# A graph layer's node stage: rows loaded and stored two blocks at a time, and a pause behind every second early gather

## The reference

```python
h = jnp.maximum(_layernorm(x, axis=-1), 0.0)                 # x: 100000 x 64, float32
edge_in_f = concat([h[src], h[dst], edge_attr])              # 25000 edges, src random, dst sorted
msgs_f = relu(edge_in_f @ W1_f + b1_f) @ W2_f + b2_f
agg = segment_sum(msgs_f, dst, num_segments=n_nodes)
edge_in_r = concat([h[dst], h[src], edge_attr])
msgs_r = relu(edge_in_r @ W1_r + b1_r) @ W2_r + b2_r
agg = agg + segment_sum(msgs_r, src, num_segments=n_nodes)
out = x + h + relu(concat([agg, h]) @ Wn1 + bn1) @ Wn2 + bn2
```

## Time and profile before

| | us |
|---|---|
| median of 3 runs | 1609.94 |
| lowest, highest | 1607.84, 1611.34 |
| the profiled execution | 1610.51 |
| its span, first to last instruction | 1608.8 |

### The profile page before, as it was taken

The page is one execution under the profiler, slowest core; times in us unless marked ns, Lnnn a source line. Parts: engine busy times, 40 slices in busy tenths (PEclk is TensorE's granted clock), DMA queues, the critical chain, the costliest instruction groups (busy, mean ns, idle before and its releaser), DMA issues.

```text
span 1608.8 us, 29477 instructions
## 1 busy us (share of the span) xinstructions
PE 1280.4 (80%) x7070; PEld 970.6 (60%) x7070; DVE 972.0 (60%) x3294; ACT 942.1 (59%) x2256; POOL 1103.2 (69%) x1003
## 2 busy tenths in 40 slices
PE   5899998457877778887787877778888756899998
PEld 4677777335655555665565656556666544666665
DVE  7999999426666666666666666666666641222222
ACT  4888888345555555555545555555555524677776
POOL 7888888888888888888888888888888761000000
PEclk9999999768788887778778788887777887999999
DMA  6899998425555555555555555555555547999998
GB/s 214 288 312 315 312 316 290 141 51 111 109 111 111 111 105 104 104 105 105 104 104 105 105 102 100 103 103 103 104 102 101 101 71 235 345 353 343 347 342 298
DMA packets 238410, 281.00 MB, mean 175 GB/s; under 512 B 53170, under 2 KB 155200, under 8 KB 238348
## 3 DMA queue, kind: packets, MB, share of 16 engines
q1 hardware_dynamic: 168408, 241.57, 45.2%
q0 software_dynamic: 68992, 38.59, 20.5%
q10 hardware_dynamic: 948, 0.30, 0.1%
HBM read 162.62 MB, written 117.72 MB: 174 GB/s over the span
## 4 chain that ended last, share of the span: by engine, by line
POOL 33%; issue 22%; DMA 15%; PE 4%; DVE 3%; ACT 1%; POOLq 0%; SPq 0%; DVEq 0%; ACTq 0%
POOL table L532 28%; DMA out_x<-ncentred 12%; POOL got_odd L514 6%; DMA table<-to_send,scatter_at 2%; DVE ncentred L1138 2%; DVE same L979 1%; PE bank L833 1%; PE bank L871 1%; DMA same<-table 1%; PE bank L820 1%; PE bank L882 0%; PE bank L818 0%; SPq L392 0%; PE bank L804 0%; PE bank L892 0%
## 5 line engine op out<-in xcount | busy, mean ns | idle before, releaser
L532 POOL DMA_INDIRECT table<-to_send,scatter_at x392 | 622.6, 1588 | 134.0 <-issue 118.4
L846 PEld LDWEIGHTS bank<-message,same 128*128 128x128 f32 x1960 | 270.3, 222 | 44.2 <-issue 39.2
L846 PE MATMUL bank<-message,same 128*128 128x128 f32 x1960 | 290.9, 313 | 4.8 <-DVE message L1011 4.8
L639 ACT ACTIVATE nh<-nx,all_sums,all_rstd 128x64 f32<-128x64 f32 x784 | 280.2, 434 | 0.1
L514 POOL DMA_INDIRECT got_even<-in_x,gather_first x196 | 212.9, 1086 | 39.8 <-issue 34.7
L775 PE MATMUL bank<-wn_h,nturned 128*128 128x256 f32 x784 | 196.7, 394 | 31.7 <-ACT nhidden L683 24.1
L514 POOL DMA_INDIRECT got_odd<-in_x,gather_at x180 | 180.2, 1001 | 54.9 <-issue 54.0
L804 PE MATMUL bank<-ident,h_ends 128*128 128x128 f32 x196 | 52.0, 359 | 198.7 <-DVE h_ends L1020 192.6
L979 DVE TENSOR_SCALAR_CACHE_REDUCE same<-others,ids 128x128 f32<-128x128 int32 (+3 forms) x392 | 190.7, 543 | 12.7 <-issue 7.9
L818 PE MATMUL bank<-turned,w_ends 128*128 128x256 f32 x392 | 167.1, 516 | 37.9 <-ACT turned_edge L609 37.9
L775 PEld LDWEIGHTS bank<-wn_h,nturned 128*128 128x128 f32 x784 | 143.1, 192 | 67.9 <-issue 36.2
(11 more groups left out here) (79 smaller groups left out, 1984.3 us busy)
## 6 DMA issues: line engine op xcount, KB each, us to landing
nx<-in_x SPq DMA_DIRECT2D x194, 256.0 KB
table<-nhidden SPq DMA_DIRECT2D x97, 512.0 KB
same<-table SPq DMA_DIRECT2D x97, 512.0 KB, 5.4
others<-numbers SPq DMA_DIRECT2D x196, 128.0 KB
out_x<-ncentred SPq DMA_DIRECT2D x97, 256.0 KB, 4.4
nx<-out_x SPq DMA_DIRECT2D x55, 256.0 KB, 4.8
out_x<-nh SPq DMA_DIRECT2D x31, 256.0 KB
table<-to_send,scatter_at POOLq DMA_INDIRECT x392
```

Of the source, the lines that this page charges most:

```text
L532: pool.indirect_dma_start(table, bass.IndirectOffsetOnAxis(ap=scatter_at[s][:, k:k + 1], axis=0), to_send[s][:, k, :], None, compute_op=AL ...
L639: last = act.activation(nh[s][:, g, :], nx[place][:, g, :], ACT.Relu, bias=all_sums[:, at, g:g + 1].rearrange("p a g -> p (a g)"), scale=a ...
L846: last = pe.matmul(bank[6 + s][:, k * M:(k + 1) * M], same[s][:, o, k * P:(k + 1) * P], message[s][:, o, :], start=(o == k), stop=(o == KB ...
```

## The change

The node stage handles two windows as one block of 2048 rows: partition p holds 16 neighbouring rows, the first 8 for the even window and the other 8 for the odd one. x of a pair is one transfer of 512 KB into one of four pair buffers (`x_pair`, the tiles `ntab` that the last stage uses for table rows), and the table rows of a pair are one transfer of up to 1 MB from one of four pair buffers (`rows_pair`, in `kept_more`). SP issues them at every second step; the load waits until both windows of the pair four pairs back are centred, the store until both windows of its pair are copied. `nx` is no longer used in the node stage, so the first two loads of the edge stage lose their wait. The first pair of x is loaded in two halves, both ahead of the list `src`. In the early gathers the memset and the wait for it stand only behind gathers of odd k, so 104 memsets are left, and `copy_sums` waits for 104.

```diff
+    XRING = 8
+        rows_pair = [kept_more[:, 4 * p:4 * p + 4, :].rearrange("p a c -> p (a c)") for p in range(XRING // 2)]
+        x_pair = ntab
-                Step(NW, 0).do(load_x_begin, 0, ring=NRING)
+                for s in range(2):
+                    load_window(x, 0, s, x_pair[0][:, s * G * D:(s + 1) * G * D], b_x_first if s == 0 else b_x[0])
...
+            def pair_rows(a, i):
+                rows = a[(NW - 2) * WIN:N, :] if is_last(i) else a[bass.ds(i * (2 * WIN), 2 * WIN), :]
+                return rows.rearrange("(p h g) d -> p h (g d)", h=2, g=G)
...
             def load_x_begin(i, s, turn, place):
                 if not first(turn):
-                    sp.wait_ge(b_centred[s], i - 1)
-                load_window(x, i, s, flat(nx[place]), b_x[place])
+                    for q in range(2):
+                        sp.wait_ge(b_centred[q], i - XRING // 2 + 1)
+                sp.dma_start(x_pair[place // 2][0:parts(i), :], pair_rows(x, i).rearrange("p h c -> p (h c)")
+                             ).then_inc(b_x[place // 2], 16)
...
-            def store_rows(i, s):
-                sp.wait_ge(b_rows[s], 2 * (i + 1))
-                store_window(table[0:N, :], i, s, nhidden[s][:, :], b_stored[s])
+            def store_rows(i, s, turn, place):
+                for q in range(2):
+                    sp.wait_ge(b_rows[q], 2 * (i + 1))
+                sp.dma_start(pair_rows(table[0:N, :], i).rearrange("p h c -> p (h c)"),
+                             rows_pair[place // 2][0:parts(i), :]).then_inc(b_stored[place // 2], 16)
...
             def begin(w):
-                w.do(load_x_begin, 6, ring=NRING)
+                if w.n % 2 == 0:
+                    w.do(load_x_begin, XRING, ring=XRING)
...
-                w.do(store_rows, -1)
+                if w.n % 2 == 0:
+                    w.do(store_rows, -2, ring=XRING)
...
                     else:
                         continue
+                    if k % 2 == 0:
+                        continue
                     if pauses:
                         pool.wait_ge(s_paused, pauses)
                     pool.memset(idle, 0.0).then_inc(s_paused, 1)
...
-                    act.wait_ge(s_paused, KB * (PAIRS + LOOK))
+                    act.wait_ge(s_paused, KB // 2 * (PAIRS + LOOK))
...
-                    if not first(i):
-                        act.wait_ge(b_stored[s], 16 * i)
-                    act.copy(nhidden[s][:, half * 512:(half + 1) * 512], bank[2 + 2 * s + half][:, :]
-                             ).then_inc(b_rows[s], 1)
+                    if not first(turn):
+                        act.wait_ge(b_stored[place // 2], 16 * turn)
+                    c = (2 * s + half) * 512
+                    act.copy(rows_pair[place // 2][:, c:c + 512], bank[2 + 2 * s + half][:, :]).then_inc(b_rows[s], 1)
```

More of the change, by code:

```diff
@@ L111, in gnn_layer @@
     MORE_FROM = KEPT - MORE
-    assert NW % 2 == 0 and N % G == 0 and G * D == 2 * KB * D and 2 * KEPT <= PAIRS and 4 * KEPT <= NB
+    assert NW % 2 == 0 and N % (2 * G) == 0 and G * D == 2 * KB * D and 2 * KEPT <= PAIRS and 4 * KEPT <= NB
     table = nc.dram_tensor("table", (ROWS, M), F32, kind="Internal").ap()
@@ L255, in gnn_layer @@
         s_loads_held = sem("loads_held")
-        b_x = [sem(f"b_x_in{p}") for p in range(NRING)]
+        b_x = [sem(f"b_x_pair_in{p}") for p in range(XRING // 2)]
+        b_x_first = sem("b_first_x_in")
         b_sums = sems("b_sums_ready")
@@ L269, in gnn_layer @@
         b_rows = sems("b_rows_ready")
-        b_stored = sems("b_rows_stored")
+        b_stored = [sem(f"b_rows_pair_stored{p}") for p in range(XRING // 2)]
         e_means = sem("e_scaled_means_ready")
@@ L334, in set_up @@
                     sp.dma_start(wn1_h[half * D:(half + 1) * D, half, :], Wn1[M:M + D, :]).then_inc(s_wn1h, 16)
-                for k in range(1, 6):
-                    Step(NW, 0).do(load_x_begin, k, ring=NRING)
+                for k in range(2, XRING, 2):
+                    Step(NW, 0).do(load_x_begin, k, ring=XRING)
                 param(w1_ends[:, 1, :], W1_f[0:2 * D, :])
@@ L371, in load, with is_last, parts @@
                                  ).then_inc(s_others[s], 16)
[L373 to L380, removed]
+            def is_last(i):
+                return isinstance(i, int) and i == NW // 2 - 1
+            def pair_rows(a, i):
+                rows = a[(NW - 2) * WIN:N, :] if is_last(i) else a[bass.ds(i * (2 * WIN), 2 * WIN), :]
+                return rows.rearrange("(p h g) d -> p h (g d)", h=2, g=G)
+            def parts(i):
+                return LASTP if is_last(i) else P
             def load_window(a, i, s, to, landed):
[L383 to L386, removed]
+                sp.dma_start(to[0:parts(i), :], pair_rows(a, i)[:, s, :]).then_inc(landed, 16)
             def store_window(a, i, s, of, stored):
[L389 to L392, removed]
+                sp.dma_start(pair_rows(a, i)[:, s, :], of[0:parts(i), :]).then_inc(stored, 16)
             def flat(a):
@@ L527, in scatter @@
                     pool.wait_ge(s_table0, 16)
-                    for q in range(2):
-                        pool.wait_ge(b_stored[q], 16 * (NW // 2))
+                    for q in range(XRING // 2):
+                        pool.wait_ge(b_stored[q], 16 * len(range(q, NW // 2, XRING // 2)))
                 pool.sem_inc(s_scatters_begun, 1)
@@ L678, in copy_rows, with copy @@
             def copy_rows(half):
-                def copy(i, s):
+                def copy(i, s, turn, place):
                     act.wait_ge(b_product[s], i + 1)
-                    if not first(i):
-                        act.wait_ge(b_stored[s], 16 * i)
-                    act.copy(nhidden[s][:, half * 512:(half + 1) * 512], bank[2 + 2 * s + half][:, :]
-                             ).then_inc(b_rows[s], 1)
+                    if not first(turn):
+                        act.wait_ge(b_stored[place // 2], 16 * turn)
+                    c = (2 * s + half) * 512
+                    act.copy(rows_pair[place // 2][:, c:c + 512], bank[2 + 2 * s + half][:, :]).then_inc(b_rows[s], 1)
                 return copy
@@ L692, in begin @@
                     square(0, 0)
-                w.do(copy_rows(0), -1)
-                w.do(copy_rows(1), -1)
+                w.do(copy_rows(0), -1, ring=XRING)
+                w.do(copy_rows(1), -1, ring=XRING)
             for k in range(3):
@@ L1053, in of_window, with x_window @@
                 return a[:, bass.ds(2 * i + s, 1), :].rearrange("p a g -> p (a g)")
+            def x_window(place):
+                half = place % 2
+                return x_pair[place // 2][:, half * G * D:(half + 1) * G * D].rearrange("p (g d) -> p g d", d=D)
             def sum_begin(i, s, turn, place):
-                dve.wait_ge(b_x[place], 16 * (turn + 1))
-                dve.tensor_reduce(of_window(all_sums, i, s), nx[place][:, :, :], AX.X, ALU.add).then_inc(b_sums[s], 1)
+                if first(turn) and place == 0:
+                    dve.wait_ge(b_x_first, 16)
+                else:
+                    dve.wait_ge(b_x[place // 2], 16 * (turn + 1))
+                dve.tensor_reduce(of_window(all_sums, i, s), x_window(place), AX.X, ALU.add).then_inc(b_sums[s], 1)
             def centre_begin(i, s, turn, place):
@@ L1085, in begin @@
             def begin(w):
-                w.do(sum_begin, 3, ring=NRING)
+                w.do(sum_begin, 3, ring=XRING)
                 w.do(variance_begin, 2)
-                w.do(centre_begin, 3, ring=NRING)
+                w.do(centre_begin, 3, ring=XRING)
                 w.do(invert_begin, 2)
@@ L1097, in _ @@
             for k in range(3):
-                Step(NW, 0).do(sum_begin, k, ring=NRING)
-                Step(NW, 0).do(centre_begin, k, ring=NRING)
+                Step(NW, 0).do(sum_begin, k, ring=XRING)
+                Step(NW, 0).do(centre_begin, k, ring=XRING)
                 if k == 0:
```

14 lines of the change are left out of this document (6 added, 8 removed).

## The result

The changed kernel takes 1832.18 us (median of 4, 1813.46 to 1840.14) against 1608.89 us before: a ratio of 1.137, 95% interval 1.128 to 1.146. The forecast was 1582 us, range 1571 to 1599. The profiled execution took 1840.14 us, its span is 1838.0.

The account below looks back on a forecast made before the run. GpSimd, running back to back, was taken as the bound: early gathers, then scatters. Memsets 17.7 us plus fewer delayed gathers 10.9, less a later start 0.5, gave 28.1 us off, hence 1582 us; range 1571 to 1599.

Parts of the forecast that it names:

- rival (c): Node stage: without the pause a pair's second gather is held up by transfers, costing 30 us, 1640; chance 8%.
- the sum's: Whole kernel: 28.1 us won, first scatter near 312.6, edge stage moving as a block, 1582 us.
- the floor: First scatter's earliest start: sums at 301.90 plus 1.44 us from copy to scatter, 303.3; at most 37.4 us won.
- the memsets' term: Early gathers on GpSimd: 104 of 208 memsets go, 0.17 us each, 17.7 us won, bounds 12 and 37.
- rival (a): Early gathers: only the memsets' plain price is won, gathers caught as often as today; 17 us, 1593; chance 20%.
- The delayed gathers: Early gathers slowed by VectorE's two-input operations: some 35 to 45 instead of 69, 10.9 us less (2 to 19).
- the walk: Early gathers' starts laid one by one on VectorE's two-input operations: delay 31 us today, 15 to 17 with new spacing.
- Zero for all of these: Loads and stores by pairs, with their waits: nothing won or lost, node stage stalls up to 9 us covered.

## Why the prediction was wrong

**What held.** The first gather moved by 0.59 us (7.81 to 8.40; 0.5 was said, 0.48 in the run of the pairs alone), but that shows little: in the kernels whose start is that of before it lies between 7.55 and 8.26. The idle between the gathers of a pair is 0.30, a pair takes 2.70 (83.03 to 85.73 is the next pair's start; 2.73 was said), 104 memsets are left, and no gather behind the first took over 1.48 us: rival (c), which had the right side, put the loss on the second gather of a pair and its transfers, and at 1640; neither was the mechanism or the size.

**The step that failed** is the sum's: "the first scatter starts near 312.6, still later than the floor of 303.3". The floor took the sums' 301.90 as given, whatever the gathers do. The prediction knew one direction of influence only, VectorE slowing the gathers, and priced the gathers' rate by what GpSimd gains from it. The other direction, gathers holding up TensorE, isn't in the rows of a kernel whose memsets keep it small; in the changed kernel TensorE's updates came 20.9 us late in the median, the sums at 524.8 and the first scatter at 531.49. What was in the trace of before was a trace of it: 6 late updates out of 140, three of them at the very floor, among them that of the first batch's join, which ended at 301.90 and whose update came at 303.42. I had not read the updates, and the memset itself, an operation whose result nobody reads, I priced as lost time without asking what its absence would let through.

**A bound of the memsets' term** was added up wrong: with 1.02 for both gathers of a pair it takes 1.02 + 0.30 + 1.02 + 0.49 = 2.83, so 104 x 0.07 = 7 us are won and not 12, and the upper end of rival (a) is 1603 instead of 1598. The outcome does not hang on it.

**The delayed gathers:** 7 were slow, not 35 to 45, and the list ended 41.6 us earlier instead of 28. That is no success of the walk: VectorE stood still, so there was nothing to collide with. In the run with halved memsets twice as wide, where it ran, 64 were slow.

**"Zero for all of these"**, the loads and stores by pairs, failed by 39 us: the working followed them through the node stage, where it held (they are hidden, and the stage even gets 10 us shorter), and took everything behind the first scatter as a block that moves. But `load_window` and `store_window` serve the last stage too, which has no cover: 28 us for the last pair's 106 partitions, some 8 to 10 for the gaps. The edge stage itself was nearly rigid (994.8 in the changed kernel, 991.4 with the pairs alone, 988.0 with the last pair put back, 988.3 before).

**What stays open.** By what way a gather holds up TensorE's updates. The runs show that the rate of gathers decides, not their rows, nor that two are neighbours, and that TensorE is hit hardest: ScalarE's updates came in time in every run, VectorE's in all but the two without the last 24 memsets (three in the kernel before, two of up to 1.9 us in the pairs), GpSimd's own memset updates were late at times (up to 3.84 us in the changed kernel; with the tiny memsets 52 of 78 by over 0.5). A gather of 64 rows has in common with one of 128 that it raises its semaphore by 16 (`then_inc(landed, 16)`), which no run changed. The Trainium skill, page "VectorE: DVE Perf Modes", section "The TRN2 errata — SBUF-src ops pay a fixed extra latency per instruction", warns that semaphore increments at a high rate from one engine can deadlock another, and that kernels with dense increments on completion from several engines should space them. Nothing deadlocked here, and no run shows whether it is the same thing; that spacing helps agrees with the table above.

## What to carry to other kernels

An operation without a use for its result, with a wait of its own, may be a brake: before it is taken away, read how late the other engines' semaphore updates come beside it, and try it in the stretch where nobody waits for the engine that would be held up, with an eye on how long the delay lasts behind it (12 us past the last fast gather here). When a helper for loads or stores changes, follow every stage that calls it; the one bound by transfers pays for gaps between the pieces and, here, for 106 partitions.

## What the runs showed of the hardware that I had not expected

- Indirect gathers issued by GpSimd every 1.36 us or faster delay TensorE's semaphore updates by 11 to 33 us in the median and by up to 60; every 1.40 us by 2.8 in the median; every 1.45 us between 1 of 161 and 25 of 145, in four kernels, by over 0.5. TensorE goes on with later matmuls in the meantime.
- A gather of 64 rows takes GpSimd 0.91 us, one of 128 rows 0.96.
- Transfers over 106 partitions left the DMA engines busy 0.13 of the time at the end, as 2 of 16 would; they cost 28 us for one pair of windows in the last stage.
- Loads and stores of single windows with gaps between their pieces run at 331 GB/s, without gaps at 345.
